# Second projection's first value tiles moved into the first attention's program, its first head's values moved between the second head's tiles, and the FFN's remainders moved ahead of additions

## What is computed

```python
x = x + attn(cond(x, ...), w_qkv, w_dense)          # 32 heads, 8 key/value heads, head size 128, causal over 32 tokens
x = x + ffn(cond2(x, Wq, Wk, Wv, Wo, ..., k_cache, v_cache, block_table, cache_seqlens))

def attn(q, w_qkv, w_dense):
    qkv = q @ w_qkv.T                                # 4096 + 1024 + 1024 columns
    ...
    probs = softmax(where(causal, qh @ kh.T * scale, min))
    return (probs @ vh) @ w_dense.T

def cond2(x, ...):
    q, k, v = x @ Wq.T, x @ Wk.T, x @ Wv.T
    q, k = rope(rmsnorm(q, q_norm_w), pos), rope(rmsnorm(k, k_norm_w), pos)
    ...                                              # attention over 512 cached and 32 new keys
    return o @ Wo.T

def ffn(x, lora_A, lora_B, W, bias, lora_weights):
    return x @ W.T + bias + lora_out                 # LoRA of 8 x rank 16
```

## Time and profile before

| | |
|---|---|
| median of 3 runs | 1652.56 us (1652.09 to 1655.01) |
| the profiled execution | 1651.88 us, of which the span of the trace is 1650.1 us |
| mean granted TensorE clock | 0.998 of full speed |
| TensorE (PE) busy | 1598.4 us |
| PEld busy | 1395.1 us |
| DVE busy | 1107.2 us |
| ACT busy | 940.8 us |
| POOL busy | 304.2 us |
| longest wait of PE in `gqa` | 2.8 us, at its start |
| PE's wait at the start of `cached_qkv` | 2.4 us |
| PE's wait at the start of `cached_attention` | 1.4 us |
| PE's wait at the start of the FFN | 1.4 us |

### The profile page before, as it was taken

How to read it: one execution, slowest core, us unless ns; L and a number is a source line. 1 busy time by engine, 2 the same in 40 slices (tenths; PEclk the granted TensorE clock), 3 DMA queues, 4 the chain that set the end, 5 groups by cost and what they waited for, 6 DMA issues and landing times. The chain is left out here.

```text
span 1650.1 us, 33861 instructions
## 1 busy us (share of the span) xinstructions
PE 1598.4 (97%) x10728; PEld 1395.1 (85%) x10728; DVE 1107.2 (67%) x2937; ACT 940.8 (57%) x2396; POOL 304.2 (18%) x306
## 2 busy tenths in 40 slices
PE   2899999999999999999999999999999999999998
PEld 2787888888888788888879999999999999977777
DVE  8504544554355777777748999999999999764443
ACT  3224223232322276666758999999999999822221
POOL 1000000000000155655711112112111211022210
PEclk9999999999999999999999999999999999999999
DMA  6621222202210234343669999999999999595401
GB/s 229 215 96 49 71 71 70 70 0 70 70 64 26 81 131 135 110 133 112 195 209 284 324 309 297 324 309 305 308 318 314 296 324 307 178 313 153 124 3 51
DMA packets 230098, 290.73 MB, mean 176 GB/s; under 512 B 17658, under 2 KB 181914, under 8 KB 221850
## 3 DMA queue, kind: packets, MB, share of 16 engines
q1 hardware_dynamic: 220826, 222.90, 43.0%
q0 software_dynamic: 9216, 67.11, 11.4%
HBM read 237.44 MB, written 50.41 MB: 174 GB/s over the span
## 5 line engine op out<-in xcount | busy, mean ns | idle before, releaser
L1615 PE MATMUL p_val<-probs_t,vals 128*128 128x128 f32 x2048 | 271.3, 276 | 0.0
L1615 PEld LDWEIGHTS p_val<-probs_t,vals 128*128 128x128 f32 x2048 | 248.7, 192 | 0.1
L1524 DVE CUSTOM_DVE_ANT_0 probs<-p_score,mask 128x544 f32<-128x544 f32 x256 | 184.3, 720 | 41.9 <-issue 34.8
L1428 ACT ACTIVATE probs<-probs,low 128x544 f32<-128x544 f32 x256 | 190.2, 743 | 0.7 <-DVE low L1524 0.6
L1513 DVE TENSOR_TENSOR wo_lo<-keys,wo_hi 128x544 fp32r<-128x544 f32 x224 | 161.8, 722 | 0.2 <-ACT wo_hi L1423 0.2
L459 PE MATMUL p_tile<-w_hi,y_hi 128*128 128x512 f32 x384 | 157.1, 409 | 2.4 <-PEq L472 2.4
L1436 ACT ACTIVATE probs_t<-p_turn 128x512 f32<-128x512 f32 x256 | 148.9, 582 | 16.8 <-PE p_turn L1594 16.7
L1594 PE MATMUL p_turn<-cst,probs 128*128 128x128 f32 x1024 | 153.4, 272 | 0.7 <-ACT probs_t L1436 0.7
L1423 ACT ACTIVATE wo_hi<-keys 128x544 fp32r<-128x544 f32 x224 | 145.8, 651 | 14.2 <-PE p_score L461 14.0
L1099 POOL TENSOR_TENSOR w_lo<-w_raw,w_hi 128x512 fp32r<-128x512 f32 x44 | 57.1, 1300 | 524.1 <-DVE w_hi L1134 506.8
L459 PE MATMUL p_score<-wo_hi,q_hi 128*128 128x272 f32 x448 | 149.6, 334 | 2.4 <-DVE low L1524 1.2
(11 more groups left out here) (218 smaller groups left out, 3540.6 us busy)
## 6 DMA issues: line engine op xcount, KB each, us to landing
keys<-in_k_pages SPq DMA_DIRECT2D x512, 128.0 KB
qk_new<-x_res SPq DMA_DIRECT2D x80, 256.0 KB, 2.2
x_res<-qk_new SPq DMA_DIRECT2D x32, 512.0 KB
o_new<-x_res SPq DMA_DIRECT2D x32, 512.0 KB, 6.5
w_raw<-in_w_vkq_t SPq DMA_DIRECT2D x12, 1024.0 KB, 5.6
w_raw<-in_w_qkv_t SPq DMA_DIRECT2D x10, 1024.0 KB, 8.4
toep<-kpad SPq DMA_DIRECT2D x32, 256.0 KB, 4.4
w_raw<-in_w_dense_t SPq DMA_DIRECT2D x8, 1024.0 KB, 5.5
```

The lines of the kernel that those rows point to most:

```text
L1428: nc.scalar.activation(probs[:, i % 8, :], probs[:, i % 8, :], ACT.Exp, bias=low[:, i % 4:i % 4 + 1], scale=-1.0, accum_out=total[:, i % 4 ...
L1524: v.tensor_tensor_reduce(out=probs[:, i % 8, :], in0=score_at(i % 2, slice(0, KEYS)), in1=mask[:, i // HK, :], scale=1.0, scalar=3e38, op0 ...
L1615: mm = pe.matmul(p_val[:, h, half * P:(half + 1) * P], vals[slot][:, c // RUN, c % RUN * HK * D + k * D:c % RUN * HK * D + (k + 1) * D], p ...
```

## The change

Four edits.

The scores' PSUM tensor, now `p_first`, is allocated ahead of the programs and shared by `gqa` and `cached_qkv`. After its last product tile TensorE makes the first two value tiles of the second projection in `gqa` (`EARLY = 2`), into `p_first`; `cached_qkv` skips them, and its four tiles of PSUM are `p_first` and two more banks, in turn.

The first head's second scores go behind head 1's tile 0, its first values behind tile 1; ScalarE's rounding of these values goes behind its copy of tile 1, and VectorE normalises the second half ahead of the first values' remainders.

SP's loads of the first head's weights go behind the store of value tile 1, the load of its dense weights behind that of tile 7.

In the last head of `output_ffn` the remainders 0 to 3 of `y3` go ahead of additions 4 to 7.

```diff
 # gqa, SP
-            sp.dma_start(w_raw[:, :, 0:E], w_qkv[:, :, 0:E]).then_inc(w_in, 16)
-            sp.dma_start(w_raw[:, :, E:5 * D], w_qkv[:, :, HQ * D:HQ * D + D]).then_inc(w_in, 16)
-            sp.dma_start(wd_raw[:, :, :], w_dense[:, 0:G, :]).then_inc(wd_in, 16)
             for t in range(VT):
+                if t == 2:
+                    sp.dma_start(w_raw[:, :, 0:E], w_qkv[:, :, 0:E]).then_inc(w_in, 16)
+                    sp.dma_start(w_raw[:, :, E:5 * D], w_qkv[:, :, HQ * D:HQ * D + D]).then_inc(w_in, 16)
+                if t == TT:
+                    sp.dma_start(wd_raw[:, :, :], w_dense[:, 0:G, :]).then_inc(wd_in, 16)
                 sp.wait_ge(proj_taken, t + 1)
 # gqa, ScalarE
                     if second(k):
                         if i == 0:
                             exponentials(0, 1)
+                        if i == 1:
+                            split_values(0, 0)
...
                 if first:
-                    split_values(k, 0)
                     return
 # gqa, VectorE
                     centre(k, 1)
+                    normalise(k, 1, first)
                     split_values(k, 0)
-                    normalise(k, 1, first)
                     split_values(k, 1)
 # gqa, TensorE
+                    if second(k) and i == 1:
+                        pe.wait_ge(proj_taken, VT + QT)
+                        scores(0, 1, True)
+                    if second(k) and i == 2:
+                        values(0, 0, True)
                     if second(k) and i == 4:
                         values(0, 1, False)
...
                 if first:
-                    pe.wait_ge(proj_taken, k * QT + VT + QT)
-                    scores(k, 1, first)
-                    values(k, 0, first)
                     return
...
             for i in range(OT):
                 product_tile(HK - 1, i, final=True)
+            pe.wait_ge(w_lo_ready, EC * (HK + 1))
+            pe.wait_ge(x_lo_ready, EC)
+            pe.wait_ge(unfolded, 2 * HK)
+            for t in range(EARLY):
+                at = slice(t * P, (t + 1) * P)
+                for c in range(EC):
+                    last_mm = three_pass(pe, p_first[:, t, :], y_hi[:, c, at], y_lo[:, c, at],
+                                         w_hi[:, c, 0:E], w_lo[:, c, 0:E], c == 0, c == EC - 1)
+                last_mm.then_inc(tables.tile_done, 1)
 # cached_qkv
-        p_tile = ctx.enter_context(nc.psum_tensor("p_tile", [P, 4, E], F32))
+        p_tile = (p_first, ctx.enter_context(nc.psum_tensor("p_tile", [P, 2, E], F32)))
...
             def project(m, i):
                 t = m * PAIR + i
+                if isinstance(t, int) and t < EARLY:
+                    return
 # output_ffn, VectorE
                     for i in range(OT):
+                        if last and slot == 1 and i >= EC:
+                            split_y(i - EC)
                         v.wait_ge(out_done, OT * k + i + 1)
...
-                        if last and slot == 1:
-                            if i < EC:
-                                v.wait_ge(ffn_hi_ready, 1)
-                                v.tensor_tensor(w_lo[:, 0, i, :], w_ffn[:, i, :], w_hi[:, 0, i, :].bitcast(F32), ALU.subtract).then_inc(ffn_lo_ready, 1)
-                            else:
-                                split_y(i - EC)
+                        if last and slot == 1 and i < EC:
+                            v.wait_ge(ffn_hi_ready, 1)
+                            v.tensor_tensor(w_lo[:, 0, i, :], w_ffn[:, i, :], w_hi[:, 0, i, :].bitcast(F32), ALU.subtract).then_inc(ffn_lo_ready, 1)
```

More of the change, by code:

```diff
@@ L461, in three_pass, with gqa @@
     return pe.matmul(out, a_lo, b_hi, start=False, stop=stop)
-def gqa(nc, io, cst, x_res, y_hi, y_lo, weights, tables):
+def gqa(nc, io, cst, x_res, y_hi, y_lo, weights, tables, p_first):
     with ExitStack() as ctx:
@@ L488, in gqa @@
         p_proj = ctx.enter_context(nc.psum_tensor("p_proj", [P, 2, E], F32))
-        p_score = ctx.enter_context(nc.psum_tensor("p_score", [P, 2, 4, P], F32))
+        p_score = p_first[:, :, :].rearrange("p f (b n) -> p f b n", b=4)
         p_val = ctx.enter_context(nc.psum_tensor("p_val", [P, 4, 4, P], F32))
@@ L848 @@
 LAG = 3
+EARLY = 2
 class PageTables:
@@ L875, in __init__ @@
         self.v_stored = [sem(f"v3_stored{i}") for i in range(2)]
+        self.tile_done = sem("tile_done")
         self.pages_ready = sem("pages_ready")
@@ L937, in make_rows, with cached_qkv @@
                         ALU.mult, ALU.add).then_inc(self.rows_ready, 1)
-def cached_qkv(nc, io, cst, x_res, x_hi, x_lo, weights, tables):
+def cached_qkv(nc, io, cst, x_res, x_hi, x_lo, weights, tables, p_first):
     with ExitStack() as ctx:
@@ L973, in cached_qkv @@
         lo_piece = sem("lo_piece")
-        tile_done = sem("tile_done")
+        tile_done = tables.tile_done
         tile_taken = sem("tile_taken")
@@ L1048, in take_values @@
                     act.wait_ge(v_stored[i % 2], 16 * (w // 2))
-                nc.scalar.activation(v_out[:, i % 2, :], p_tile[:, i % 4, :], ACT.Copy).then_inc(tile_taken, 1)
+                nc.scalar.activation(v_out[:, i % 2, :], p_tile[i // 2 % 2][:, i % 2, :], ACT.Copy).then_inc(tile_taken, 1)
             def split_hi(n, slot, c):
@@ L1078, in body @@
                     for h in range(4):
-                        ins = nc.scalar.activation(squared[:, h, :], p_tile[:, i % 4, h * D:(h + 1) * D], ACT.Square,
+                        ins = nc.scalar.activation(squared[:, h, :], p_tile[i // 2 % 2][:, i % 2, h * D:(h + 1) * D], ACT.Square,
                                                    accum_out=squares[:, i % 4, h:h + 1])
@@ L1169, in scale_and_rotate @@
                     inv = inv_rms[:, i % 4, h:h + 1]
-                    head = p_tile[:, i % 4, h * D:(h + 1) * D]
+                    head = p_tile[i // 2 % 2][:, i % 2, h * D:(h + 1) * D]
                     v.scalar_tensor_tensor(out=part_a[:, i % 4, h, :], in0=head, scalar=inv, in1=rot[:, key, 0, i % TT, :],
@@ L1193, in project @@
                 for c in range(EC):
-                    mm = three_pass(pe, p_tile[:, i % 4, :], x_hi[:, c, rows], x_lo[:, c, rows],
+                    mm = three_pass(pe, p_tile[i // 2 % 2][:, i % 2, :], x_hi[:, c, rows], x_lo[:, c, rows],
                                     w_hi[:, i // TT, c, :], w_lo[:, i // TT, c, :], c == 0, c == EC - 1)
@@ L1934, in build @@
             weights = Weights(ctx2, nc)
+            p_first = ctx2.enter_context(nc.psum_tensor("p_first", [P, EARLY, E], F32))
             ssm_conv(nc, io, cst, x_res, y_hi, y_lo, weights, tables.keys_0)
-            gqa(nc, io, cst, x_res, y_hi, y_lo, weights, tables)
+            gqa(nc, io, cst, x_res, y_hi, y_lo, weights, tables, p_first)
             tables.place_out(ctx, nc)
             tables.place_values(ctx, nc)
-            cached_qkv(nc, io, cst, x_res, y_hi, y_lo, weights, tables)
+            cached_qkv(nc, io, cst, x_res, y_hi, y_lo, weights, tables, p_first)
         wo = OutputWeights(ctx, nc)
```

## The result

| | before | changed |
|---|---|---|
| median | 1652.32 us (8 runs, 1649.72 to 1655.68) | 1656.11 us (8 runs, 1654.58 to 1657.56) |
| the profiled execution | 1651.88 us, span 1650.1 | 1655.17 us, span 1653.4 |
| ratio to before | | 1.0024, 95% interval 1.0015 to 1.0033 |

The changed kernel is slower by 0.24%, some 4 us (2.5 to 5.5). 1657.8 had been forecast, with a range of 1653.0 to 1660.5, and 0.72 for slower by over 0.2%. That it is slower is clear; whether it is by over 0.2% the interval leaves open.

What follows compares the result with a forecast made beforehand. TensorE, busy 97% of the span, was taken as the bound. Loads 0, head +2.5, early tiles +2.7, remainders -1.6 and one clock fall +1.65 gave +5.25 us on the median 1652.56: 1657.8 us, range 1653.0 to 1660.5.

Steps and rivals of the forecast that it cites:

- Loads of the first head: First value tiles: loads moved behind stores cost 0 to +0.5 us, taken as 0; tile 2's store lands late.
- First head: Ahead of head 1: the wait for weights stays, now empty, and the moved scores and values cost +2.5 us.
- Early value tiles: Second projection's start: TensorE's hole shrinks, but other engines start 3.35 us later, so the first turn comes +2.7 us later.
- the chain: From the second program's start through ScalarE, SP's load and store, and POOL to TensorE's first turn; shifted by 3.35 us.
- the wait for tile 7's copy: Second projection: TensorE's tile 11 waits for ScalarE's copy of tile 7, 583.4 against 582.4.
- Last remainders: Step into the FFN: fourth remainder done a tile earlier, step 1.83 us becomes about 0.24, so -1.6 us.
- Clock: Behind the two new idle stretches of TensorE: one fall of the granted clock counted, +1.65 us.
- Sum: Whole kernel: +3.6 us before the clock, +5.25 us with one fall of it.
- the faster one: Second projection: tile 5's store lands after 2.0 us, moved tiles earn about -2.0, total -1.1, 1651.5 us; chance 0.12.

Runs made afterwards that it cites:

- e10: Kernel before with the first head's scores and values moved, plus 15 useless matmuls ahead of TensorE's wait for head 1's weights; ratio 1.0014.
- e7: Kernel before with only the first values moved behind head 1's tile 1, scores left ahead of head 1; ratio 1.0012.
- e4: Kernel before with only SP's first loads moved behind value stores; ratio 1.0001.
- e1: Kernel before with only the FFN's remainders moved ahead of the last additions; ratio 0.9988.
- e2: Kernel before with only the first head's scores and values moved; ratio 1.0029.
- e6: Kernel before with two early value tiles, and SP's load of the third weight chunk ahead of its wait for tile 4's copy; ratio 0.9997.
- e3: Kernel before with only the two early value tiles moved into the first attention's program; ratio 1.0010.
- e5: Changed kernel with the first head's scores and values put back; ratio to the kernel before 1.0010.
- e11: Kernel before with two early value tiles and the FFN remainders moved, without SP's moved loads or the moved head; ratio 1.0004.

## Why the prediction was right

- **Loads of the first head**: 0 forecast, 0.2 measured alone (-1.2 to +1.7). The store of tile 2 landed late as worked out and TensorE didn't notice.
- **First head**: +2.5 forecast. The wait kept its 4.25 us and the inserted work cost 2.6 us with the clock held up (e10), with no wait ahead of the second values. The step held: a wait that hid work for nothing was emptied.
- **Early value tiles**: the mechanism held, the size was off. +2.7 was forecast, and the profile has 36.87 - 35.59 = +1.3. The hole at the barrier shrank to 0.71, the other engines started late, tile 5's store took 6.7 us to let ScalarE go on, and TensorE waited for POOL. The mis-sized term is the chain, which was shifted by 3.35 us as it stood: SP's issue of the 1 MB load took 0.43 us here instead of the 1.81 of the earlier trace rows, and the chain is shorter by that 1.4 (so is the wait for tile 7's copy, which vanished). I had taken the 1.81 for a property of the load. The trace of the kernel before says otherwise: of the ten loads of this line, shortest, median and longest in ns,

```profile
L1003 SPq DMA_DIRECT2D w_raw<-in_w_vkq_t x10: 394/400/1808, 570.9 to 807.2; - x10
```

  it was the one long issue. The experiments whose second projection starts as before had 1.62 (e7), 1.32 (e4) and 0.43 or 0.44 us (e1, e2, e10) for this same load, and all eight kernels with early tiles 0.43 to 0.45. So it differs between executions. A large DMA just ahead of it is not the reason: in e6 the load was issued 0.5 us behind a store of the residual (564.63 and 564.16) and took 0.45 us. What makes it long stays open.
- **Last remainders**: -1.6 forecast, -1.59 in the profile, -2.0 (-3.5 to -0.5) alone.
- **Clock**: one fall was counted at +1.65. The profile has one, behind the idle head, and it cost 26.26 - 24.77 = 1.5. Behind the first turn the clock didn't fall in this execution, but it did in three others with the same wait (e3, e5, e11). One fall of two was a choice between rows that disagreed, and that the profiled execution has exactly one is luck. Over the eight executions the mean granted clock was 0.9958, against 0.9972 of the kernel before: an estimate of 2.3 us, at most, lost to falls beyond those of before.
- **Sum**: 2.6 + 1.5 + 1.3 - 1.6 = 3.8 us by these distances (the whole span grew by 3.3), 4.0 by the ratio, against 5.25 forecast; the 1.4 us of the load's issue is the difference to the distances. The range had 7.5 us and so left room for an error of this size.
- **Rivals**: the faster one named the right lever. In e6 the store landed without the load ahead of it and the early tiles gained 35.59 - 33.97 = 1.6 us at the boundary. It was given -2.0 and needs the load moved, which the change doesn't do.

## What to carry to other kernels

Before moving work out of a wait, ask what set the wait's length: if it was another engine's work that does not move, what stood in the wait was free and is now paid. Work that one engine does ahead of a barrier delays every other engine's start by its length, so the longest chain from the barrier to that engine's next need has to be followed, DMAs that share its queue among them, before the hole counts as a gain. Moving a large load one place ahead of small stores that someone waits for can be worth more than the move itself. And a duration taken from a single row has to be compared with the other instructions of its line before it goes into a sum: the 1.81 us that made the forecast 1.4 us too high was the longest of ten.

## What the runs showed of the hardware that was not expected

- The granted clock fell after TensorE's idle time in some executions and not in others with the same idle time: the old hole of 2.44 us ahead of the second projection left it at 1.00 in the kernel before, e4, e7 and e10, while in e1, with that hole unchanged, the stretches read

```profile
550.00:553.40 3.40, 1.28 (x6) 1.00 0.00 0
553.60:556.80 3.20, 3.07 (x7) 0.50 0.00 0
```

  and the boundary took 37.09 instead of 35.59 us. In e2 it fell there too (37.20). A fall cost 1.5 to 2.8 us of TensorE's time at each place. Executions of the kernel before lie between 1649.58 and 1657.03 us; a fall more or less can be a good part of that, though no run separates it. So the distances in the trace, not the ratios, carry the small terms here.
- The same DMA instruction of 1 MB took SP 1.81, 1.62, 1.32 or 0.43 us to issue in four executions of kernels whose second projection starts alike (before, e7, e4, e10).
